# First attention: both value products of a pair of units issued in the odd step

## The chip, the cores and the metric

The kernel runs on one core of one Trainium2 chip. The metric is the device time of one execution in microseconds (us), the median of several runs. One execution is recorded by the profiler; its span runs from its first to its last instruction. TensorE is PE in the profile (PEld is its loading of weights), VectorE DVE, ScalarE ACT, GpSimd POOL and SyncE SP.

## The reference, cut to what matters

Two layers over x of shape (8, 16, 16, 192). The first is window attention with 12 heads of 16 and relative positions, and an MLP; the second causal attention with 3 heads and a soft mixture of 4 experts. The change lies in the window attention:

```python
attn = jnp.einsum('bqc,bkc->bqk', q * scale, k)
attn = (attn.reshape(-1, WS, WS, WS, WS) + rel_h[:, :, :, :, None] + rel_w[:, :, :, None, :]).reshape(-1, N, N)
attn = jax.nn.softmax(attn, axis=-1)
out = jnp.einsum('bqk,bkc->bqc', attn, v)
```

Each image of 16 x 16 tokens is padded to 28 x 28 and cut in windows of 14 x 14, so one window is full of real tokens and the three others hold two border strips and padding.

## The kernel before

The first attention is `body_a`, a loop of 4 iterations over pairs of images (`PAIRS`), between 44 and 310 us of the span. An iteration computes relative position terms and v, and then goes through 18 units (`UNITS`): 12 main ones (`MAIN`), each two heads of one image's full window (scores of 112 x 784 for four parts), and 6 border ones (two heads of both images' border, 128 x 512). Two units make a pair d; there are 9.

Every engine has its own order of the steps u; the engines meet by semaphores alone. TensorE does in step u, in this order:

- the scores of unit u (`scores_full`, L1105, or `scores_border`, L1113) into banks 0 and 1 or 2 and 3, once the exponentials of unit u-2 are done (a_p);
- the transposes of the exponentials of unit u-2 (L1207) into banks 4 and 5, once ScalarE has copied the transposes of the unit before out of them (a_pta);
- in the first three iterations, from step 18 on, query and key products of the next iteration (L222): queries in 18, 19 and 20, keys in 20;
- value products of pair d with the transposed exponentials as moving operand (`values(d, n)`, L1125 for main units, L1128 and L1131 for border ones), accumulated into bank 6 or 7. The half n adds one unit's share for both of its heads; main and border halves have 4 and 6 matmuls in the program (8 and 12 in the trace, where a matmul of f32 shows twice). The last one counts a_o up;
- in steps 5, 9 and 13 transposes of normalized tokens for the next iteration (`front_turn_part`, L1085 and L1089); the last of them only if there is one.

ScalarE does in step u the copy of unit u-2 from banks 4 and 5 to one of four buffers `pts` (L902), and then the exponentials of unit u (L912), 4 or 2 instructions; after them, in steps 5, 9 and 13, it moves the turned tokens out (L845, L849). VectorE does in step u the maxima of unit u (L638), in even steps the reciprocal of pair (u-6)/2 (`sums`, L607), in odd ones the scaling of pair (u-7)/2 (`scaled`, L620 to L626), which sets bank 6 or 7 free (a_on), and a share of the next tokens' split. Pair d is given to VectorE by a_o, and ScalarE's copy of unit v waits for a_o of pair v/2 - 2, because it reuses that buffer.

Before its value products a pair waits for v (d = 0), for the copies of both of its units, for its bank (from d = 2), and for turned tokens moved out of bank 7 (d = 1, 3, and 5 where there is a next iteration). After the last step come, in the first three iterations, two more key products, and then the projection (L1256, L1257), VectorE's residual and the next iteration.

Of the kernel before, what the change touches and what calls it, by code (L numbers as in the profile page):

```python
# [37 lines left out]
OUTS = UNITS // 2  # L38
# [30 lines left out]
def build(nc, x, xe, wall0, wall1, rel, wp, w2a, w2e, bias_cols, bias_rows, b2r, c_ident, c_keys,  # L69
          c_border, c_mask, out):  # L70
    with ExitStack() as ctx:
# [3 lines left out]
        def sem(name):  # L75
            return ctx.enter_context(nc.semaphore(name))
# [29 lines left out]
        def views(spec):  # L106
# [74 lines left out]
        ln_mv, ln_rstd, ln_xn, ln_tr, ln_tr_e, ln_xt, ln_xt_e, ln_hi, ln_split = (  # L181
            sem(n) for n in ("ln_mv", "ln_rstd", "ln_xn", "ln_tr", "ln_tr_e", "ln_xt", "ln_xt_e", "ln_hi", "ln_split"))

        a_q, a_k, a_v, a_qraw, a_ka, a_kb, a_ve, a_kae, a_rel, a_qa = (
            sem(n) for n in ("a_q", "a_k", "a_v", "a_qraw", "a_ka", "a_kb", "a_ve", "a_kae", "a_rel", "a_qa"))
# [3 lines left out]
        a_s, a_nm, a_p, a_t, a_pta, a_o, a_own, a_on = (  # L189
            sem(n) for n in ("a_s", "a_nm", "a_p", "a_t", "a_pta", "a_o", "a_own", "a_on"))  # L190
# [34 lines left out]
        def xcols(a, b):  # L225
            return [xs[:, k, a:b] for k in range(3)]
# [10 lines left out]
        def unit(u):  # L237

            if u < MAIN:
                return QR, 2, 2 * QT, u // HP, u % HP  # L240
            return P, 1, EKEYS, None, u - MAIN
# [20 lines left out]
        def gated(eng, n):  # L262

            eng.sem_inc(gate[n], 1)
# [799 lines left out]
        def _(pe):  # L1064
# [52 lines left out]
            def values(d, n):  # L1117

                rows, parts, keys, i, h = unit(2 * d)
                at, vc = n * parts * rows, slice(n * 3 * HD, n * 3 * HD + 4 * HD)  # L1120
                for k in range(2) if parts == 2 else ((2, 0, 1), (0, 1, 2))[n]:
                    for p in range(2):
                        o, turned = ps[64 * p:64 * p + 64, 6 + d % 2, :], pts[(2 * d + p) % 4]
                        if parts == 2:
                            last = mm(o[:, 0:2 * QR], ve[0:QT, 2 * i + k, h + p, vc], turned[0:QT, k, at:at + 2 * QR],  # L1125
                                      start=n + k == 0, stop=n + k == 2)
                        elif k == 2:
                            last = mm(o[:, 0:P], vee[:, 2, h + p, vc], turned[:, 1, at:at + P], start=n == 0, stop=n == 1)  # L1128
                        else:
                            part = slice(64 * k, 64 * k + 64)  # L1130
                            last = mm(o[:, part], vee[:, k, h + p, vc], turned[:, 0, at + 64 * k:at + 64 * k + 64],  # L1131
                                      start=False, stop=False)
                return last

            def queries(g):

                product(ps[:, g, :], (CQ + g * P, CQ + g * P + P), xcols(0, N)).then_inc(a_q, 1)
# [5 lines left out]
            def body_a(it, nxt):  # L1143

                pe.wait_ge(o_res, 1 + it * 2)

                pe.wait_ge(a_qraw, it * G + 3)
                gated(pe, 0)
                q4 = qraw.rearrange("p g (i t) -> p (g i) t", i=2)
                for step in range(4):  # L1150
                    if step == 1:
                        pe.wait_ge(a_ka, it + 1)
                        pe.wait_ge(a_kb, it * 2 + 1)
                    if step == 2:
                        pe.wait_ge(a_kb, it * 2 + 2)
                    if step:
                        gated(pe, 0)
                    for k in range(4):
                        at = 4 * step + k
                        for cols in range(2):  # L1160
                            rows = q4.rearrange("p a (y x) -> p a y x", x=W)
                            to = ps[:, REL_BANKS[cols][step], 0:384]
                            to = to.rearrange("p (a y k) -> p k a y", k=4, a=2 * G)[:, k] if cols else \
                                to[:, 96 * k:96 * k + 96]
                            last = mm(to, relt[:, W * cols + at, :],  # L1165
                                      rows[:, :, :, at] if cols else rows[:, :, at, :], start=True, stop=True)
                    last.then_inc(a_rel, 1)

                pe.wait_ge(a_xw, it * 3 + 3)
                for i in range(2):  # L1170

                    pe.wait_ge(a_qw, it * 4 + 1 + 2 * i)
                    gated(pe, 0)
                    for t in range(2):
                        at = N + P + (2 * i + t) * QT
                        last = product(ps[0:QT, V_BANKS[i], t * D:t * D + D], (CV, CV + D), xcols(at, at + QT), True)
                    last.then_inc(a_v, 1)
                pe.wait_ge(a_qa, it * 4 + 3)
                gated(pe, 0)
                product(ps[:, V_BANKS[2], 0:D], (CV, CV + D), xcols(N, N + P), True).then_inc(a_v, 1)  # L1180
                base = it * UNITS
                for u in range(UNITS + 4):
                    if u < UNITS:
                        rows, parts, keys, i, h = unit(u)
                        if u == 0:

                            pe.wait_ge(a_qa, it * 4 + 4)
                            pe.wait_ge(a_qw, it * 4 + 4)
                        if u >= 2:

                            pe.wait_ge(a_p, base + u - 1)
                        if u == MAIN:

                            pe.wait_ge(a_kae, it * 2 + 2)
                            pe.wait_ge(a_qb, it * 2 + 2)
                        gated(pe, 0)
                        (scores_full(u, i, h) if u < MAIN else scores_border(u, h)).then_inc(a_s, 1)
                    if 2 <= u < UNITS + 2:
                        v = u - 2
                        rows, parts, keys, i, h = unit(v)  # L1200
                        half = keys // 2

                        pe.wait_ge(a_p, base + v + 1)
                        pe.wait_ge(a_pta, 1 + base + v)
                        for k in range(2):
                            for n in range(UH * parts):
                                last = tr(ps[0:half, 4 + k, n * rows:n * rows + rows],  # L1207
                                          pp[0:rows, v % 3, n, k * half:k * half + half], ident[0:rows, 0:rows])
                        last.then_inc(a_t, 1)
                    if nxt and UNITS <= u < UNITS + G:  # L1210

                        if u == UNITS:
                            pe.wait_ge(ln_split, it + 2)
                        queries(u - UNITS)
                    if nxt and u == UNITS + 2:

                        pe.wait_ge(a_p, base + UNITS)
                        keys_of(0)
                    if u >= 4:
                        d, n = (u - 4) // 2, (u - 4) % 2  # L1220
                        if n == 0:
                            if d == 0:

                                pe.wait_ge(a_ve, it * 6 + 6)

                            pe.wait_ge(a_pta, 1 + base + 2 * d + 2)
                            if d >= 2:
                                pe.wait_ge(a_on, it * OUTS + d)

                            if d in (1, 3):  # L1230
                                pe.wait_ge(ln_xt, 2 * it + 3 + d // 2)
                            if nxt and d == 5:
                                pe.wait_ge(ln_xt_e, it + 2)
                            gated(pe, 0)
                        last = values(d, n)
                        if n:
                            last.then_inc(a_o, 1)
                    if u in ((5, 9, 13) if nxt else (5, 9)):

                        if u > 5:  # L1240
                            pe.wait_ge(a_on, 1 + it * OUTS + u // 2 - 2)
                        front_turn_part(it + 1, u // 4 - 1, (ln_xt_e, it + 1))

                if nxt:

                    pe.wait_ge(a_pta, 1 + base + UNITS)
                    for g in (1, 2):
                        keys_of(g)
                pe.wait_ge(a_on, 1 + it * OUTS + OUTS)
                project(0, (6, 7))  # L1250
# [154 lines left out]
            for w in range(CUNITS):  # L1405
                it, u = divmod(w, CU)
# [262 lines left out]
```

## Time and profile before

| | |
|---|---|
| median of 3 runs | 916.26 us (914.36 to 916.26) |
| the profiled execution | 910.88 us |
| its span | 909.0 us, mean granted clock of TensorE 0.992 |
| TensorE busy | 836.4 us, 92% of the span |
| VectorE, ScalarE, GpSimd busy | 459.0, 461.3 and 180.4 us |
| TensorE in the chain that ended last | 75% |

Busy shares are those of the whole span; the first attention takes less than a third of it. In timelines a line is a run of like instructions, with its start, its length (the end of a group of matmuls is modelled and lies some hundredths past the start of the next group), and in square brackets the idle time of the engine before it and what ended that.

### The profile page before, as it was taken

How to read it: one execution, taken by the hardware profiler on the slowest of the kernel's cores; microseconds unless marked ns; L12 is line 12 of the kernel's file. 1: busy time of each engine (PE TensorE's matmuls, PEld its weight loads, DVE VectorE, ACT ScalarE, POOL GpSimd, SP SyncE). 2: the span in 40 equal slices, each digit the busy share in tenths (PEclk: the TensorE clock that was granted, in tenths of full speed). 3: DMA queues.
4: the chain of work that ended last, by engine and by line, in shares of the span. 5: the costliest groups of instructions: out<-in, count | busy, mean ns of one | idle time of the engine just before them, and what ended most of it. 6: DMA issues, size and time to landing. Idle time of an engine off the chain costs nothing.

```text
span 909.0 us, 14872 instructions
## 1 busy us (share of the span) xinstructions
PE 836.4 (92%) x5384; PEld 675.3 (74%) x5384; DVE 459.0 (50%) x1025; ACT 461.3 (51%) x945; POOL 180.4 (20%) x257
## 2 busy tenths in 40 slices
PE   1989989989989899989988999989999899989998
PEld 1866866766776687878877599966998589975988
DVE  4878688688687643366655410264004530163001
ACT  5887677678578443246645333354343342453232
POOL 3050040031010022236302500034001420034000
PEclk9999999999999999999998999999999999999999
DMA  7010000000000000001003000000000000000000
GB/s 203 1 40 2 1 27 12 0 12 23 0 1 1 27 12 23 12 24 45 16 1 121 1 1 0 5 14 0 0 0 17 0 0 0 0 18 1 1 1 17
DMA packets 12710, 15.48 MB, mean 17 GB/s; under 512 B 5312, under 2 KB 10560, under 8 KB 12544
## 3 DMA queue, kind: packets, MB, share of 16 engines
q1 hardware_dynamic: 10656, 9.46, 3.4%
q0 software_dynamic: 2016, 5.51, 2.2%
q8 instruction: 24, 0.39, 0.2%
q14 instruction: 14, 0.11, 0.0%
HBM read 13.39 MB, written 1.57 MB: 16 GB/s over the span
## 4 chain that ended last, share of the span: by engine, by line
PE 75%; DVE 12%; ACT 5%; issue 5%; DMA 1%; SPq 0%; POOL 0%; DVEq 0%; ACTq 0%; POOLq 0%
PE ps L222 20%; PE ps L1554 14%; PE ps L1481 6%; PE ps L1207 5%; PE ps L1569 5%; PE ps L1125 4%; PE ps L1299 4%; PE ps L1105 3%; DVE area L276 2%; ACT area L912 2%; PE ps L1113 2%; PE ps L1085 1%; DVE dstat L772 1%; PE ps L1165 1%; PE ps L1511 1%
## 5 line engine op out<-in xcount | busy, mean ns | idle before, releaser
L222 PE MATMUL ps<-xs,ws 128*128 128x512 f32 x460 | 124.9, 416 | 5.7 <-DVE xs L503 3.7
L1554 PE MATMUL ps<-area 128*128 128x192 f32 x768 | 127.4, 326 | 0.0
L1554 PEld LDWEIGHTS ps<-area 128*128 128x128 f32 x768 | 124.8, 190 | 2.1 <-issue 0.5
L222 PE MATMUL ps<-ws,wx 128*128 128x512 f32 x480 | 116.1, 397 | 1.2 <-DVE ws L793 1.2
L1053 ACT ACTIVATE area<-ps,bcol 128x512 f32<-128x512 f32 x96 | 65.7, 688 | 86.6 <-PE ps L222 86.6
L804 DVE TENSOR_TENSOR area<-ps,area 128x384 f32<-128x384 f32 x32 | 17.9, 558 | 177.8 <-PE ps L1554 177.7
L222 PEld LDWEIGHTS ps<-ws,wx 128*128 128x128 f32 x480 | 89.3, 188 | 22.6 <-DVE ws L793 3.0
L222 PEld LDWEIGHTS ps<-xs,ws 128*128 128x128 f32 x460 | 86.0, 196 | 24.1 <-issue 6.4
L912 ACT ACTIVATE area<-ps,nm 112x196 f32<-112x196 f32 (+1 forms) x240 | 85.6, 440 | 19.5 <-DVE nm L638 19.5
L415 POOL TENSOR_TENSOR area<-area,dstat 128x512 f32<-128x512 f32 x32 | 32.9, 1040 | 271.4 <-DVE dstat L769 271.4
L638 DVE TENSOR_REDUCE nm<-ps 112x4 f32<-112x784 f32 (+1 forms) x72 | 62.7, 874 | 26.8 <-PE ps L1105 21.7
L1207 PE MATMUL ps<-ident,area 112*98 112x112 f32 (+1 forms) x480 | 63.0, 271 | 1.0 <-ACT room L902 0.7
L1207 PEld LDWEIGHTS ps<-ident,area 112*98 112x98 f32 (+1 forms) x480 | 46.6, 131 | 21.4 <-issue 15.0
L1481 PE MATMUL ps<-area,xn 128*128 128x512 f32 x128 | 57.5, 597 | 5.1 <-DVE area L785 4.1
L1105 PE MATMUL ps<-area 64*112 64x196 f32 x384 | 44.0, 350 | 15.5 <-ACT area L912 13.6
L607 DVE RECIPROCAL room<-ps 128x224 f32<-128x224 f32 (+1 forms) x36 | 48.6, 1351 | 12.8 <-PE ps L1128 12.6
L1105 PEld LDWEIGHTS ps<-area 64*112 64x112 f32 x384 | 30.3, 175 | 26.9 <-issue 26.9
L1481 PEld LDWEIGHTS ps<-area,xn 128*128 128x128 f32 x128 | 23.4, 190 | 31.6 <-issue 31.6
L421 POOL TENSOR_TENSOR area<-area 128x512 f32<-128x512 f32 x32 | 39.6, 1280 | 34.8 <-DVE area L785 34.8
L1569 PE MATMUL ps<-area 128*128 128x193 f32 x256 | 42.7, 326 | 0.0
L1569 PEld LDWEIGHTS ps<-area 128*128 128x128 f32 x256 | 42.1, 190 | 0.0
L902 ACT ACTIVATE area<-ps 98x896 f32<-98x896 f32 (+1 forms) x40 | 31.6, 791 | 18.8 <-PE ps L1207 18.7
(177 smaller groups left out, 1373.7 us busy)
## 6 DMA issues: line engine op xcount, KB each, us to landing
stage<-in_wall POOLq DMA_DIRECT2D x42, 128.0 KB, 2.4
area<-in_w2e SPq DMA_DIRECT2D x1, 2304.0 KB, 8.3
out<-xres SPq DMA_DIRECT2D x4, 384.0 KB, 2.6
xres<-in_x SPq DMA_DIRECT2D x1, 1152.0 KB, 7.8
area<-in_wall SPq DMA_DIRECT2D x2, 512.0 KB, 5.7
area<-in_w2a SPq DMA_DIRECT2D x1, 576.0 KB, 3.7
room<-in_rel SPq DMA_DIRECT2D x4, 128.0 KB, 5.7
xres<-in_x SPq DMA_DIRECT2D x1, 384.0 KB, 3.2
```

The costliest lines, as they stand in the source:

```text
L222: last = mm(out_, l, r, start=n == 0, stop=n == len(pairs) - 1)
L421: nc.gpsimd.tensor_tensor(ct[:, s, :], ct[:, s, :], bc, ALU.add).then_inc(d_cs, 1)
L607: V.reciprocal(den[:, d % 2, 0:n], ps[:, 6 + d % 2, 0:n]).then_inc(a_own, 1)
L638: V.tensor_reduce(nm[0:rows, u % 2, 0:UH * parts], ps[0:rows, b0:b0 + UH, 0:parts * keys].rearrange("p h (t k) -> p h t k", k=keys), AX.X, ...
L912: last = A.activation(pp[0:rows, u % 3, k, 0:keys], ps[0:rows, UH * (u % 2) + k // parts, c0:c0 + keys], ACT.Exp, bias=nm[0:rows, u % 2, k ...
L1053: A.activation(hTd[:, m, :], ps[:, (e * MC + m) % 4, :], ACT.Gelu_apprx_tanh, bias=bcol[:, E1B + e * MC + m:E1B + e * MC + m + 1]).then_in ...
L1105: last = mm(ps[0:QR, UH * (u % 2) + k, 2 * QT * t:2 * QT * t + 2 * QT], qs[q, 2 * operands(h) + i, QR * t:QR * t + QR], keys, start=True, ...
L1125: last = mm(o[:, 0:2 * QR], ve[0:QT, 2 * i + k, h + p, vc], turned[0:QT, k, at:at + 2 * QR], start=n + k == 0, stop=n + k == 2)
L1207: last = tr(ps[0:half, 4 + k, n * rows:n * rows + rows], pp[0:rows, v % 3, n, k * half:k * half + half], ident[0:rows, 0:rows])
L1481: last = mm(ps[:, 4 * h + 2 * b + part, :], xn[:, 2 * b + j, part * P:part * P + P], dd[:, b, j, 512 * h:512 * h + 512], start=j == 0, sto ...
L1554: last = mm(ps[:, 4 + b, s * D:s * D + D], hTd[:, m, b * T + s * P:b * T + s * P + P], w2x[:, e * MC + m, :], start=m == 0, stop=m == MC - 1)
L1569: last = mm(ps[:, 6 + n // 2, (n % 2) * (D + 1):(n % 2 + 1) * (D + 1)], ct[:, s, n * P:n * P + P], yy[:, n // 2, s, :], start=s == 0, stop ...
```

## The change

TensorE's value products of a pair stood in two steps: the first half in step 2d + 4, the second in step 2d + 5. Now both stand in step 2d + 5, behind that step's transposes, with the waits that stood before the first half. The even steps from 4 to 20 hold no value products. Other engines' programs are not touched.

```diff
--- before.py
+++ after.py
@@ -1216,25 +1216,23 @@
 
                         pe.wait_ge(a_p, base + UNITS)
                         keys_of(0)
-                    if u >= 4:
-                        d, n = (u - 4) // 2, (u - 4) % 2
-                        if n == 0:
-                            if d == 0:
-
-                                pe.wait_ge(a_ve, it * 6 + 6)
-
-                            pe.wait_ge(a_pta, 1 + base + 2 * d + 2)
-                            if d >= 2:
-                                pe.wait_ge(a_on, it * OUTS + d)
-
-                            if d in (1, 3):
-                                pe.wait_ge(ln_xt, 2 * it + 3 + d // 2)
-                            if nxt and d == 5:
-                                pe.wait_ge(ln_xt_e, it + 2)
-                            gated(pe, 0)
-                        last = values(d, n)
-                        if n:
-                            last.then_inc(a_o, 1)
+                    if u >= 5 and u % 2:
+                        d = (u - 5) // 2
+                        if d == 0:
+
+                            pe.wait_ge(a_ve, it * 6 + 6)
+
+                        pe.wait_ge(a_pta, 1 + base + 2 * d + 2)
+                        if d >= 2:
+                            pe.wait_ge(a_on, it * OUTS + d)
+
+                        if d in (1, 3):
+                            pe.wait_ge(ln_xt, 2 * it + 3 + d // 2)
+                        if nxt and d == 5:
+                            pe.wait_ge(ln_xt_e, it + 2)
+                        gated(pe, 0)
+                        values(d, 0)
+                        values(d, 1).then_inc(a_o, 1)
                     if u in ((5, 9, 13) if nxt else (5, 9)):
 
                         if u > 5:
```

## Rows read from the trace of the kernel before

**Rows 1.** Windows, second iteration: stretch, us, busy PE, PEld, DVE, ACT, POOL, clock, DMA.

```profile
116.00:126.00 10.00, 6.12 (x60) 4.71 (x57) 9.63 (x26) 5.80 (x15) 5.15 (x10) 1.00 0.00 0
126.00:161.00 35.00, 34.49 (x330) 22.34 (x329) 28.88 (x42) 28.48 (x64) 8.22 (x16) 1.00 0.09 25
```

**Rows 2.** Timeline, TensorE, second iteration, steps 10 and 11: start us, us, engine, line.

```profile
141.60 0.65 PE L1085 MATMUL ps<-ident,xn 128*128 128x128 f32 x4 [0.16 <-DVE area L620]
142.18 0.92 PE L1105 MATMUL ps<-area 64*112 64x196 f32 x8
143.03 0.97 PE L1207 MATMUL ps<-ident,area 112*98 112x112 f32 x8
143.93 0.98 PE L1125 MATMUL ps<-room 98*64 98x224 f32 x8
144.84 0.92 PE L1105 MATMUL ps<-area 64*112 64x196 f32 x8
145.69 0.97 PE L1207 MATMUL ps<-ident,area 112*98 112x112 f32 x8
```

**Rows 3.** Timeline, ScalarE, second iteration, the copies of steps 10 and 11.

```profile
144.12 0.92 ACT L902 ACTIVATE area<-ps 98x896 f32<-98x896 f32 x1 [0.71 <-PE ps L1207]
...
146.70 0.92 ACT L902 ACTIVATE area<-ps 98x896 f32<-98x896 f32 x1 [0.41 <-PE ps L1207]
```

**Rows 4.** Timeline, VectorE, second iteration, step 10.

```profile
143.15 0.97 DVE L638 TENSOR_REDUCE nm<-ps 112x4 f32<-112x784 f32 x1 [0.96 <-PE ps L1105]
144.04 1.55 DVE L607 RECIPROCAL room<-ps 128x224 f32<-128x224 f32 x1
```

**Rows 5.** Timeline, TensorE, second iteration, step 4.

```profile
124.81 0.92 PE L1105 MATMUL ps<-area 64*112 64x196 f32 x8 [0.24 <-ACT area L912]
...
126.57 0.98 PE L1125 MATMUL ps<-area,room 98*64 98x224 f32 x8
```

**Rows 6.** Timeline, ScalarE, second iteration, exponentials of steps 2 and 3.

```profile
123.27 1.39 ACT L912 ACTIVATE area<-ps,nm 112x196 f32<-112x196 f32 x4
...
125.85 1.37 ACT L912 ACTIVATE area<-ps,nm 112x196 f32<-112x196 f32 x4 [0.33 <-DVE nm L638]
```

**Rows 7.** Timelines, first and last iteration: values of step 4, exponentials of step 3.

```profile
54.70 0.98 PE L1125 MATMUL ps<-area,room 98*64 98x224 f32 x8
...
53.53 1.37 ACT L912 ACTIVATE area<-ps,nm 112x196 f32<-112x196 f32 x4
...
269.86 0.98 PE L1125 MATMUL ps<-area,room 98*64 98x224 f32 x8
...
268.71 1.36 ACT L912 ACTIVATE area<-ps,nm 112x196 f32<-112x196 f32 x4
```

**Rows 8.** Timeline, TensorE, second iteration, steps 14, 17 and 18.

```profile
152.68 0.66 PE L1113 MATMUL ps<-area 64*64 64x256 f32 x8
153.27 0.66 PE L1207 MATMUL ps<-ident,area 128*128 128x128 f32 x4
154.11 0.98 PE L1125 MATMUL ps<-room 98*64 98x224 f32 x8 [0.18 <-issue]
...
159.48 0.66 PE L1207 MATMUL ps<-ident,area 128*128 128x128 f32 x4
...
160.91 0.30 PE L1207 MATMUL ps<-ident,area 128*128 128x128 f32 x1 [0.17 <-ACT room L902]
```

**Rows 9.** Timeline, ScalarE, second iteration, copies of steps 14 and 17.

```profile
154.05 0.60 ACT L902 ACTIVATE area<-ps 128x512 f32<-128x512 f32 x1 [0.19 <-PE ps L1207]
...
160.17 0.60 ACT L902 ACTIVATE room<-ps 128x512 f32<-128x512 f32 x1 [0.30 <-PE ps L1207]
```

**Rows 10.** Timelines, last iteration: TensorE's step 19, VectorE's reciprocal of pair 7.

```profile
304.92 0.63 PE L1207 MATMUL ps<-ident,area 128*128 128x128 f32 x4 [0.18 <-ACT area L902]
...
306.20 0.96 DVE L607 RECIPROCAL room<-ps 128x128 f32<-128x128 f32 x1 [0.53 <-PE ps L1128]
```

**Rows 11.** Timeline, TensorE, first iteration, scores of step 2.

```profile
47.34 1.59 PE L1105 MATMUL ps<-area 64*112 64x196 f32 x8 [2.00 <-ACT area L912]
```

## The prediction

> **What bounds the kernel now.** I read the windows first. Inside the step loop of the first attention (126 to 161 us, second iteration) TensorE is busy 34.49 of 35 us at granted clock 1.00, VectorE 28.88 and ScalarE 28.48; in the ten microseconds ahead of it, where the loop fills, TensorE has 6.12 of 10 [rows 1]. So from step 4 on this stage goes at TensorE's pace, and anything that stops TensorE there is added to the time.
>
> The timeline of TensorE comes next. It shows what a step is made of: in steps 10 and 11 of the second iteration scores take 0.85 us (142.18 to 143.03), the transposes 0.90, half a pair of value products 0.91, then the next scores at once [rows 2]. Two steps are 2 x 2.66 = 5.32 us without idle time. The reader is to look at what fills the distance between one group of transposes and the next: values 0.91 and scores 0.85. All transposes write banks 4 and 5, and the transposes of unit v wait (a_pta) until ScalarE has copied unit v-1 out of these banks. The ScalarE timeline says when that is: the copy starts 1.09 us after the transposes start (143.03 to 144.12) or 1.01 (145.69 to 146.70), and lasts 0.92 [rows 2, 3]. What a copy costs up to the next transposes shows where TensorE already waits for one: copy at 160.17, 0.60 long, transposes at 160.91, so 0.14 us from its end [rows 8, 9].
>
> **The change.** Arithmetic, data and buffers stay. The same 8 + 8 value matmuls of each of the 9 pairs are issued together in the odd step; no transfer moves, and the queues of SP and POOL are not touched. Signals a_o come at the same place of the order. Per pair one half moves from between the even step's transposes and the odd step's scores to behind the odd step's transposes. The even step becomes 0.85 + 0.90 = 1.75 us, the odd one 0.85 + 0.90 + 1.82 = 3.57. No new wait is written, but an old one starts to bind.
>
> *Transposes of steps 7, 9, 11.* From the start of the even step's transposes, TensorE reaches the odd ones after 0.90 + 0.85 = 1.75 us. The copy allows them after 1.01 to 1.09, plus 0.92, plus 0.14 = 2.07 to 2.15. Wait 0.32 to 0.40, I take the middle, 0.36: these are two kinds of copy that alternate, and which falls in the even step I leave open. 3 per iteration, 4 iterations: 12 x 0.36 = 4.32 (3.84 to 4.80). Behind the waiting transposes stand both halves of the values, the token transposes and the next scores. VectorE waits for those scores: it starts its maximum 0.97 us after they start (142.18 to 143.15), and then has a reciprocal of 1.55 [rows 2, 4]. ScalarE waits for the transposes. Neither becomes the limit: both had about 6 of 35 us free and the stage gets longer.
>
> *Step 13.* The scores of the border units (step 12 on) take 0.59 (152.68 to 153.27) [rows 8], but the transposes of step 12 are still of the long kind with the long copy: 0.90 + 0.59 = 1.49 against 2.07 to 2.15. Wait 0.58 to 0.66, 4 times: 2.48 (2.32 to 2.64).
>
> *Steps 15 and 17.* Transposes 0.59, scores 0.59: 1.18. The border copy starts 0.78 (153.27 to 154.05) or 0.69 (159.48 to 160.17) after its transposes and lasts 0.60: 0.78 or 0.69 + 0.60 + 0.14 = 1.52 or 1.43 [rows 8, 9]. Wait 0.25 to 0.34, 8 times, taken 0.295: 2.36 (2.00 to 2.72). In step 19 of the first three iterations a query product lies between, and nothing waits.
>
> *Step 5.* Here ScalarE still sets the pace. Its exponentials are followed by the scores that need their bank: started 123.27, 1.39 long, scores at 124.81, so duration + 0.15 [rows 5, 6]. The scores of step 5 need the exponentials that start at 125.85 and last 1.37: they may start at 127.37. Now the first value half runs from 126.57 and fills this time; without it TensorE stands from 126.57: 0.80 us. In the third iteration all is the same to 0.01 us. In the first, 53.53 + 1.37 + 0.15 = 55.05 against 54.70: 0.35; in the last, 268.71 + 1.36 + 0.15 = 270.22 against 269.86: 0.36 [rows 7]. Sum 0.35 + 2 x 0.80 + 0.36 = 2.31.
>
> *End of the last iteration.* No queries follow there. The transposes of step 19 wait for a copy as now (0.18 idle before 304.92), and the half of pair 7 that now runs ahead of them in this gap comes after them: its reciprocal at 306.20 is on the chain that ends the stage, so it is later by the length of that half. A half of this kind runs in step 17 from 159.48 + 0.59 = 160.07 to 160.91 less the wait of 0.17: 0.67 [rows 8, 10].
>
> *What falls away.* Three waits of today. Step 9's token transposes wait 0.16 for VectorE (before 141.60) [rows 2]; in the new step they come a copy wait later, x4 = 0.64. Values in step 14 wait 0.18 for transposed tokens (before 154.11), in the first three iterations; the half is now in step 15: 0.54. Transposes of step 18 wait 0.17 for a copy (before 160.91); the whole pair now stands ahead of them, x4 = 0.68 [rows 8]. Together 1.86.
>
> *Joining the halves.* The trace has no two halves back to back. TensorE shows no idle time at the seams (143.03, 143.93, 144.84 follow on) [rows 2], so I take 0. Bounds: a gain of one wait like the 0.17 at each of 36 pairs, 6.1 us, and a loss of 0.04, the spread of the stall above, 1.4 us.
>
> **Sum.** 2.31 + 4.32 + 2.48 + 2.36 + 0.67 - 1.86 = 10.28 us; with the ends of the waits 9.3 to 11.3. After the loop the same instructions follow, and the phases between the iterations (projection, residual, relative terms) are chained to TensorE's last products, so the delay passes through whole. The profiled execution took 910.88 us (span 909.0): it would be 921.2. The runs shown have a median of 916.26, 5.4 us above it, and the change is added to that: **926.5 us, +1.1%**.
>
> **The clock, and a rule against it.** The new waits are many and short. In the fill phase TensorE idled nearly 4 of 10 us and kept clock 1.00 [rows 1]; in the first iteration, though, a group of scores took 1.59 us where later ones take 0.92 [rows 2, 11], which I read as the lower of the clock's two levels (1.2 and 2.4 GHz). The Trainium skill (TensorE: Matmul & The Clock Gate, A second HAM failure mode: psum-queue depth-cycling) says that TensorE idling briefly but often between groups while it cycles through PSUM banks can make the clock swing between its levels; the next rival is what it would do here. By its rule 932 us, by the rows 926.5. The loop of before already has such short waits, at clock 1.00.
>
> **Rivals.** *The clock falls.* If in each of the four iterations one group of scores and one of transposes run at the low level, at 1.59 - 0.92 = 0.67 us more each: 8 x 0.67 = 5.4, so 10.3 + 5.4 = 15.7: 932. Against it: the rows at clock 1.00 with more idle time than the change adds.
>
> *The joined halves run tighter.* At the bound above: 10.3 - 6.1 = +4.2, 920.5. For it: weights of the second half could be loaded under the first. Against it: no idle time at today's seams.
>
> *The copy hides anyway (the other side).* If the copy could follow the early transposes, because the order on ScalarE is what holds it until 1.01 to 1.09 us and the shorter even step brings its predecessor forward, the 24 copy waits would vanish: 2.31 + 0.67 - 1.86 = +1.1, 917.4, which is no measurable change. A measurement tells about 0.2% (1.8 us) from no change; this rival decides from the point where the 24 waits cost less than 0.7 us together, 0.03 each. Against it: the copy reads all eight transposes, and starts 0.1 to 0.2 us behind the last of them today. With the seam gain as well it would be faster, some 911.
>
> **Chances.** The forecast 0.73, own range 923.5 to 929.5 (its bounds, and some 2 us for the scatter of the runs, 914.36 to 916.26). Clock 0.09, tighter halves 0.08, hidden copy 0.10, of which 0.04 with the seam gain. Range 920.5 to 931.5: it leaves out the hidden copy, and about half of the clock's cases. Slower by over 0.2%: 0.90; within 0.2%: 0.06; faster: 0.04.
>
> **What would show it.** In the changed timeline: transposes in steps 7, 9, 11, 13, 15, 17 with idle time before them put down to ScalarE's copy (0.3 to 0.4, 0.6, 0.3 us); no such gap in even steps; scores of step 5 preceded by 0.8 us in the second and third iterations and 0.35 in the others; the gaps at step 9's token transposes and steps 14 and 18 gone; iteration length up by about 2.6 us; everything after the first attention of the same length. Wrong would be: copies starting well under 1 us after the transposes, value groups under 1.82 us for a pair, granted clock under 1.00 between steps 5 and 18, or VectorE named as what ends TensorE's waits.

## The result, and the profile after

The changed kernel takes 919.26 us (median of 20 runs, 914.64 to 923.55) against 916.02 us (20 runs, 910.48 to 919.88) on the same chips: ratio 1.0035, 95% interval 1.002 to 1.005. That is slower by 1.8 to 4.6 us, at the median 3.2, and not by 10.3. The direction was right; the size was three times too large, and the measured time lies below both ranges of the prediction.

The page of the changed kernel: span, busy time, and the granted clock in 40 slices.

```profile
span 917.7 us, 14872 instructions
...
PE 836.6 (91%) x5384; PEld 680.1 (74%) x5384; DVE 455.5 (50%) x1025; ACT 461.5 (50%) x945; POOL 180.4 (20%) x257
...
PEclk9999999999989889999998999999999999999999
```

Its span is 8.7 us longer than before's, more than the medians differ. The windows say why this one execution exaggerates (columns as in [rows 1]). Three stretches ran at a lower clock: the fill of the second iteration, the fill of the last one, and the end of the first attention with the products behind it. The third iteration's steps ran at 1.00.

```profile
116.00:126.00 10.00, 6.95 (x50) 5.39 (x52) 9.66 (x27) 5.13 (x14) 4.79 (x9) 0.83 0.00 0
201.00:236.00 35.00, 32.87 (x323) 22.25 (x323) 26.64 (x39) 27.18 (x61) 7.94 (x15) 1.00 0.06 17
266.00:276.00 10.00, 9.18 (x56) 6.92 (x56) 6.26 (x17) 6.81 (x17) 1.23 (x2) 0.66 0.00 0
312.00:331.00 19.00, 15.35 (x88) 12.97 (x85) 8.95 (x28) 4.91 (x7) 4.67 (x8) 0.73 0.16 46
```

The first costs little: the second iteration takes 73.07 us (116.31 to 189.38), the third 72.90. The two others cost some 2.3 us each. From its first scores to the projection the last iteration takes 53.85 us (262.28 to 316.13) against 50.35 before (259.32 to 309.67), of which 1.25 is the change (worked out further down). From the projection to the second large group of products behind it (L222) there are 26.45 us (316.13 to 342.58) against 24.04 (309.67 to 333.71). From there to the end the two executions differ by 0.2 us.

So the reading below uses the third iteration, steps 5 to 9, 12 and 13, and 14 and 15. TensorE's timeline of the changed kernel, which answers to [rows 2, 5, 8]:

```profile
201.04 0.92 PE L1105 MATMUL ps<-area 64*112 64x196 f32 x8 [0.73 <-ACT area L912]
201.89 0.97 PE L1207 MATMUL ps<-ident,area 112*98 112x112 f32 x8
202.79 1.73 PE L1125 MATMUL ps<-area,room 98*64 98x224 f32 x16
204.46 0.66 PE L1085 MATMUL ps<-ident,xn 128*128 128x128 f32 x4
205.04 0.92 PE L1105 MATMUL ps<-area 64*112 64x196 f32 x8
205.90 0.97 PE L1207 MATMUL ps<-ident,area 112*98 112x112 f32 x8
206.80 0.92 PE L1105 MATMUL ps<-area 64*112 64x196 f32 x8
208.05 0.94 PE L1207 MATMUL ps<-ident,area 112*98 112x112 f32 x8 [0.33 <-ACT area L902]
208.92 1.73 PE L1125 MATMUL ps<-room 98*64 98x224 f32 x16
210.59 0.92 PE L1105 MATMUL ps<-area 64*112 64x196 f32 x8
...
222.85 0.97 PE L1207 MATMUL ps<-ident,area 112*98 112x112 f32 x8
...
225.00 0.95 PE L1207 MATMUL ps<-ident,area 112*98 112x112 f32 x8 [0.58 <-ACT room L902]
...
228.50 0.66 PE L1207 MATMUL ps<-ident,area 128*128 128x128 f32 x4
...
230.02 0.63 PE L1207 MATMUL ps<-ident,area 128*128 128x128 f32 x4 [0.26 <-ACT area L902]
```

The reader sees all the waits that were forecast. Before the scores of step 5 (201.04) 0.73 us, before the transposes of step 7 (208.05) 0.33, of step 13 (225.00) 0.58, of step 15 (230.02) 0.26. From start to start the transposes lie 2.15 us apart (205.90 to 208.05) and 1.52 (228.50 to 230.02), both the figures of the prediction. The bracket is smaller than the loss by 0.07, because the modelled end of the group before counts as busy: 0.33 is a loss of 0.40.

What was not forecast stands between them: the joined pair takes 1.67 us (202.79 to 204.46, 208.92 to 210.59), where two halves took 2 x 0.91 = 1.82 [rows 2]. ScalarE answers to [rows 3]; its copy starts 1.09 us after the transposes at 205.90, as before:

```profile
206.99 0.92 ACT L902 ACTIVATE area<-ps 98x896 f32<-98x896 f32 x1 [1.06 <-PE ps L1207]
207.80 1.36 ACT L912 ACTIVATE area<-ps,nm 112x196 f32<-112x196 f32 x4
```

How long an iteration is shows from the first scores of one to the first of the next. Before and after, TensorE, third to fourth iteration:

```profile
187.53 1.58 PE L1105 MATMUL ps<-area 64*112 64x196 f32 x16 [0.34 <-issue]
...
259.32 1.58 PE L1105 MATMUL ps<-area 64*112 64x196 f32 x16 [0.34 <-issue]
```

```profile
189.38 1.58 PE L1105 MATMUL ps<-area 64*112 64x196 f32 x16 [0.35 <-issue]
...
262.28 1.58 PE L1105 MATMUL ps<-area 64*112 64x196 f32 x16 [0.35 <-issue]
```

71.79 us became 72.90: 1.11 more, and not the "about 2.6" of the prediction.

### The profile page after: what moved, and what is told of

The parts are those of the page before. It is cut to its first block, busy times and chain, and to the rows that moved or that the text cites. A ratio compares the mean times of both kernels' runs of the same rounds, so it can differ in the third digit from the quotient of the medians.

```text
span 917.7 us, 14872 instructions
## 1 busy us (share of the span) xinstructions
PE 836.6 (91%) x5384; PEld 680.1 (74%) x5384; DVE 455.5 (50%) x1025; ACT 461.5 (50%) x945; POOL 180.4 (20%) x257
## 4 chain that ended last, share of the span: by engine, by line
PE 74%; DVE 12%; ACT 6%; issue 5%; DMA 1%; SPq 0%; DVEq 0%; POOL 0%; ACTq 0%; POOLq 0%
PE ps L222 20%; PE ps L1552 14%; PE ps L1479 6%; PE ps L1207 6%; PE ps L1567 5%; PE ps L1125 4%; PE ps L1297 4%; DVE area L276 2%; PE ps L1105 2%; PE ps L1085 1%; DVE dstat L772 1%; ACT room L902 1%; ACT area L902 1%; PE ps L1165 1%; PE ps L1509 1%
## 5 line engine op out<-in xcount | busy, mean ns | idle before, releaser
L222 PE MATMUL ps<-xs,ws 128*128 128x512 f32 x460 | 125.8, 418 | 5.7 <-DVE xs L503 3.7
L222 PE MATMUL ps<-ws,wx 128*128 128x512 f32 x480 | 116.1, 398 | 1.2 <-DVE ws L793 1.2
L222 PEld LDWEIGHTS ps<-ws,wx 128*128 128x128 f32 x480 | 89.2, 188 | 22.7 <-DVE ws L793 3.0
L222 PEld LDWEIGHTS ps<-xs,ws 128*128 128x128 f32 x460 | 86.6, 197 | 24.5 <-issue 6.6
L1165 PE MATMUL ps<-area,room 128*128 128x96 f32 x256 | 36.4, 306 | 5.3 <-DVE xres L512 2.8
```

The lines of the kernel that those rows point to most:

```text
L222: last = mm(out_, l, r, start=n == 0, stop=n == len(pairs) - 1)
L1165: last = mm(to, relt[:, W * cols + at, :], rows[:, :, :, at] if cols else rows[:, :, at, :], start=True, stop=True)
```

## Experiments

In this section an iteration's length is again from the scores of unit 0 to those of the next iteration. Iterations in which groups ran at the lower clock (scores of 1.1 to 1.65 us in place of 0.92) are passed over where there is a like one to read. Experiments 1 to 4 ran on one chip and 5 to 8 on another, each set with its own runs of the kernel before beside it; the ratio and its interval are those on record and not the quotient of the two medians shown.

**1. Is the 0.15 us queue work at the seam?**

```diff
                         gated(pe, 0)
                         values(d, 0)
+                        gated(pe, 0)
                         values(d, 1).then_inc(a_o, 1)
```

> The changed kernel with one more semaphore increment of TensorE's queue (the gate that stands ahead of the first half) between the two halves. Theory A, the 0.15 us that a joined pair saves is the array's own start and drain of a group of another tile shape (the weights of a new group load only with its first matmul): the increment changes nothing, a main pair's values stay at 1.66 to 1.67 us from the first matmul to what follows, and the third iteration stays at 72.9 us. Theory B, the saving is queue work that the seam no longer carries: the pair is back at about 1.8 us and the iteration near 74.2 us.

Measured: third iteration 190.95 to 263.85, 72.90 us, the same to the hundredth. A semaphore instruction between the halves costs nothing. One run, 917.85 us. Theory B falls.

**2. Halves apart, but with cover between the transposes.**

```diff
-    scores(u); transposes(u - 2); values(d, 0); values(d, 1)   # odd step
+    scores(u); values(d, 0); transposes(u - 2); values(d, 1)
```

(The lines stand for the blocks of `body_a`; the waits of the pair move with its first half.)

> The changed kernel with the odd step's order scores, first half, transposes, second half: nothing in the even step, but 1.76 us of cover between any two groups of transposes again, and the halves apart. Theory A (copy waits 2.1 us per iteration, joining gains 0.15 per pair, waits before the scores of step 5 of 0.7): no waits for a copy before odd transposes, halves of 0.91, third iteration at 71.8 - 0.5 + 0.8 = 72.1 us, the whole within 1.0 to 1.003 of before. Theory C, the gain of the changed kernel comes from something else than the seam: the iteration is shorter than before's 71.8 by the amount of the gain, some 1.2 us.

Measured: 914.62 us (10 runs) against 913.96, ratio 1.0024 (1.0004 to 1.0044); third iteration 187.73 to 259.88, 72.15 us (72.1 expected): longer than before's 71.79, so the gain does not come from something else than the joining (theory C falls). TensorE's timeline, steps 6 and 7 of it (transposes are on L1223 here):

```profile
204.39 0.97 PE L1223 MATMUL ps<-ident,area 112*98 112x112 f32 x8
205.30 0.92 PE L1105 MATMUL ps<-area 64*112 64x196 f32 x8
206.15 0.98 PE L1125 MATMUL ps<-room 98*64 98x224 f32 x8
207.06 0.97 PE L1223 MATMUL ps<-ident,area 112*98 112x112 f32 x8
207.96 0.98 PE L1125 MATMUL ps<-room 98*64 98x224 f32 x8
```

No wait before 207.06, and each half takes 0.91 again. So the copy wait goes with the distance between two groups of transposes, and the saving goes with the joining.

**3. Take away the copy wait alone.**

```diff
-                        A.activation(pts[v % 4][0:half, :, 0:wide], ps[0:half, 4:6, 0:wide], ACT.Copy)\
-                            .then_inc(a_pta, 1)
+                        A.activation(pts[v % 4][0:half, 0, 0:wide], ps[0:half, 4, 0:wide], ACT.Copy).then_inc(a_ph, 1)
+                        act.wait_ge(a_t, base + v + 1)
+                        A.activation(pts[v % 4][0:half, 1, 0:wide], ps[0:half, 5, 0:wide], ACT.Copy).then_inc(a_pta, 1)
```

Transposes into bank 4 count a_th up, which the first copy waits for, and wait for a_ph; those into bank 5 go by a_t and a_pta.

> The changed kernel with ScalarE's copy cut in two, bank 4 and bank 5, each with its own signal both ways, so that transposes into bank 4 wait only for the first copy. ScalarE has one more instruction per unit (some 0.15 us more). Theory A: the waits before the transposes of steps 7 to 17 vanish, 2.1 us per iteration, third iteration at 70.8 us, whole time 8 us less than the changed kernel, 0.994 of before. Rival: ScalarE, at 28.5 of 35 us before, becomes the limit and the waits turn up before the scores instead; then the iteration stays over 72 us.

Measured: 908.85 us (10 runs) against 913.96, ratio 0.9953 (0.9933 to 0.9972). The first iteration went from 72.30 us (44.01 to 116.31) to 70.16 (44.35 to 114.51), 2.14 less. The waits before its odd transposes had cost 2.54 from start to start (brackets 2.09). Of these, 0.18 comes back because the six groups of transposes behind them take 0.90 us again and not 0.87, and 0.22 in steps 18 and 19, where transposes and queries take 2.23 us (87.91 to 90.14) after 2.01 (89.92 to 91.93 in the changed kernel). The third iteration had groups at the low clock, so the 70.8 expected of it can't be read. TensorE's steps 8 and 9, the copies between, and the window of the step loop:

```profile
65.36 0.97 PE L1210 MATMUL ps<-ident,area 112*98 112x112 f32 x8
66.26 0.92 PE L1106 MATMUL ps<-area 64*112 64x196 f32 x8
67.11 0.97 PE L1210 MATMUL ps<-ident,area 112*98 112x112 f32 x8
68.02 1.74 PE L1126 MATMUL ps<-area,room 98*64 98x224 f32 x16
```

```profile
66.06 0.54 ACT L902 ACTIVATE room<-ps 98x448 f32<-98x448 f32 x1 [0.80 <-PE ps L1210]
66.50 0.54 ACT L904 ACTIVATE room<-ps 98x448 f32<-98x448 f32 x1
```

```profile
56.00:88.00 32.00, 32.00 (x319) 21.68 (x316) 25.43 (x37) 26.99 (x73) 8.11 (x15) 1.00 0.07 21
```

TensorE has no idle time in 32 us. The two copies lie 0.44 us apart, and the first ends at 66.60, before TensorE comes back to bank 4 at 67.11. The edit does two things: the copy starts after half of the transposes (0.70 us behind their start, 65.36 to 66.06, and not 1.09), and it gives the banks back one by one. By the prediction's sum the earlier start alone would allow the transposes of steps 7, 9 and 11 after 0.70 + 0.92 + 0.14 = 1.76 us (an estimate), where TensorE needs 1.75, but not those of step 13 (1.49); no run separates the two. ScalarE, busy 26.99 of 32, is not the limit: the rival falls.

**4. First pair apart.**

```diff
+                    if u == 4:
+                        ...
+                        values(0, 0)
+                    if u == 5:
+                        values(0, 1).then_inc(a_o, 1)
-                    if u >= 5 and u % 2:
+                    if u >= 7 and u % 2:
```

> The changed kernel with the first pair's halves where they were, in steps 4 and 5; all other pairs joined. Theory A: the wait of 0.73 us before the scores of step 5 is gone and one seam of 0.15 is back: third iteration 72.9 - 0.6 = 72.3 us, whole time 2.3 us under the changed kernel, 1.001 of before. Rival: the wait only moves, because the exponentials of the fill phase set the pace whatever fills the gap: the iteration stays at 72.9.

Measured: 915.26 us (10 runs) against 913.96, ratio 1.0022 (0.9999 to 1.0045). Second iteration 115.98 to 188.28, 72.30 us, as expected, and no wait before the scores of step 5. The gap was idle time that the first half used to fill. The whole time alone would not tell this from no effect; the iteration does.

**5. A seam elsewhere.**

```diff
                         values(d, 0)
+                        if u in ((5, 9, 13) if nxt else (5, 9)):
+                            ...
+                            front_turn_part(it + 1, u // 4 - 1, (ln_xt_e, it + 1))
                         values(d, 1).then_inc(a_o, 1)
```

> The changed kernel with the token transposes of steps 5, 9 and 13 between the two halves of the pair and not behind them. The same work and waits, but one more change of tile shape in three steps of an iteration. Theory A (a seam costs 0.15 us wherever tiles of another shape follow): the third iteration, scores of unit 0 to scores of unit 0, goes from 72.90 to 72.90 + 3 x 0.15 = 73.35 us. Rival (the 0.15 is special to value halves with scores or transposes between): it stays at 72.9.

Measured: the third iteration had a group at the low clock. The first: 44.34 to 117.49, 73.15 us, against 72.30. Of the 0.85, 0.40 is something I had not expected: in step 9 the token transposes, now earlier, wait 0.33 for VectorE again, as in [rows 2]. The rest, 0.45, is three seams of 0.15. Step 5 of the third iteration shows one by itself:

```profile
205.35 0.98 PE L1125 MATMUL ps<-area,room 98*64 98x224 f32 x8
206.26 0.66 PE L1085 MATMUL ps<-ident,xn 128*128 128x128 f32 x4
206.84 0.98 PE L1125 MATMUL ps<-area,room 98*64 98x224 f32 x8
207.75 0.92 PE L1105 MATMUL ps<-area 64*112 64x196 f32 x8
```

0.91 + 0.58 + 0.91 = 2.40 us, where pair and token transposes in a row took 1.67 + 0.58 = 2.25 (202.79 to 205.04 above). One run, 920.23 us.

**6. Is the copy in two a gain by itself?** The edit of experiment 3 on the kernel before.

> The kernel before with ScalarE's copy cut in two, the halves of each pair apart as they were. Theory A (the cut helps only because the joined halves bared the copy): only the 0.17 us before the transposes of step 18 can go, third iteration 71.6 to 71.8 us, whole 0.998 to 1.001 of before. Rival (the cut is a gain by itself, worth the 0.5% that it showed with the joined halves): 0.995.

Measured: 911.91 us (10 runs) against 914.21, ratio 0.9991 (0.9959 to 1.0023); third iteration 187.41 to 259.04, 71.63 us, though two groups of scores in it took 1.16 and 1.49. No measurable gain, as the theory has it: the copy was hidden by the half that the change moved away.

**7. Everything together.** Experiments 3 and 4, and pair 7 apart in the last iteration:

```diff
+                    if not nxt and u == UNITS:
+                        pe.wait_ge(a_pta, 1 + base + 16)
+                        pe.wait_ge(a_on, it * OUTS + 7)
+                        gated(pe, 0)
+                        values(7, 0)
+                    if not nxt and u == UNITS + 1:
+                        values(7, 1).then_inc(a_o, 1)
```

> Joined halves and copy in two, with the first pair apart in every iteration (steps 4 and 5) and pair 7 apart in the last one (steps 18 and 19). Theory A: from the 0.9953 of the joined kernel with the copy in two, 0.55 us less in three iterations, 0.1 in the last and 0.5 to 0.6 at its end, together 2.3 us: 0.993 of before, third iteration 70.2 us without a clock dip. Rival (ScalarE and VectorE are the limit by now, the gaps only move): 0.995.

Measured: 908.48 us (7 runs) against 914.21, ratio 0.9926 (0.9899 to 0.9954), faster than both kernels. Second iteration 114.24 to 184.47, 70.23 us. Its interval overlaps that of experiment 3, so how much the two pairs apart add is shown by iterations only.

**8. The pair ahead of the odd transposes.**

```diff
-    scores(u); transposes(u - 2); values(d, 0); values(d, 1)   # odd step
+    scores(u); values(d, 0); values(d, 1); transposes(u - 2)
```

> The changed kernel with the joined pair ahead of the odd step's transposes. Now 2.5 us lie between even and odd transposes, and only the next scores between odd and even ones. Theory A (the wait follows from the distance of two groups of transposes, whichever step they stand in): no waits before odd transposes; waits for the copy before the transposes of step 8 (0.33 to 0.40), step 12 (0.58 to 0.66), step 16 (0.26) and step 18 (about 0.8, no scores there); none in 6 and 10, where token transposes of 0.59 lie between. Third iteration 72.5 to 73.1 us. Rival (the wait belongs to the odd units' buffers): waits stay in odd steps.

Measured: 926.19 us (one run); the third iteration had groups at the low clock (75.50 us), the second two groups of scores of 1.08 and 1.52 us, and 74.28: some 1 us over what I expected. There is no wait before odd transposes, and the copy waits before steps 8, 12, 16 and 18 are where they were forecast; one that was not forecast stands before step 14 (a bracket of 0.29 before 84.17). And there is a wait that I had missed, before the scores of odd steps. TensorE's steps 8 and 9 of the first iteration (transposes are on L1224), and ScalarE's beside them:

```profile
65.71 0.92 PE L1105 MATMUL ps<-area 64*112 64x196 f32 x8
66.88 0.94 PE L1224 MATMUL ps<-ident,area 112*98 112x112 f32 x8 [0.25 <-ACT area L902]
68.14 0.92 PE L1105 MATMUL ps<-area 64*112 64x196 f32 x8 [0.32 <-ACT area L912]
```

```profile
65.81 0.92 ACT L902 ACTIVATE area<-ps 98x896 f32<-98x896 f32 x1 [0.93 <-PE ps L1224]
66.63 1.36 ACT L912 ACTIVATE area<-ps,nm 112x196 f32<-112x196 f32 x4
```

The odd transposes now come 1.67 us later, so their copy on ScalarE (65.81) does too, and behind it in ScalarE's order the exponentials (66.63) that free the bank for the scores of step 9: 66.63 + 1.36 + 0.15 = 68.14. A late copy costs twice where something waits behind it.

## Why the prediction was wrong

The step that failed is "Joining the halves": "TensorE shows no idle time at the seams (143.03, 143.93, 144.84 follow on) [rows 2], so I take 0". The seams cost 0.15 us for each pair of main units (1.82 to 1.67), and 0.14 for a border pair (2 x 0.60 to 1.06, 234.90 to 235.96). The change joins 8 pairs of an iteration, 6 of them main, and not 9: 24 x 0.15 + 8 x 0.14 = 4.7 us, most of the 6.1 that the prediction gave as a bound for 36 pairs.

Its first sentence, that "the trace has no two halves back to back", is wrong too. In steps 20 and 21 nothing stands between the halves of pair 8, so the kernel before has a joined pair in every iteration. Here are the first half of pair 6 (step 16), and pair 8 with what follows, second iteration of the kernel before:

```profile
158.28 0.44 PE L1128 MATMUL ps<-area,room 128*64 128x128 f32 x4
...
158.88 0.66 PE L1113 MATMUL ps<-area 64*64 64x256 f32 x8
...
168.11 0.44 PE L1128 MATMUL ps<-area,room 128*64 128x128 f32 x4
168.38 0.64 PE L1131 MATMUL ps<-area,room 128*64 128x64 f32 x16
168.84 0.39 PE L1128 MATMUL ps<-area,room 128*64 128x128 f32 x4
169.16 2.58 PE L222 MATMUL ps<-xs,ws 128*128 128x512 f32 x10
```

A half alone takes 0.60 us (158.28 to 158.88), the pair 1.05 (168.11 to 169.16) and not 1.20. So the price of a seam could have been read before the change was made.

Groups of matmuls that follow on without a bracket can still hide a start-up, since the distance from start to start contains it. The engine that loads the weights fits this. Before (PEld, steps 10 and 11), and after (a joined pair, step 7 of the second iteration):

```profile
143.03 0.75 PEld L1207 LDWEIGHTS ps<-ident,area 112*98 112x98 f32 x8 [0.24 <-ACT area L912]
143.93 0.58 PEld L1125 LDWEIGHTS ps<-room 98*64 98x64 f32 x8 [0.15 <-issue]
144.84 0.60 PEld L1105 LDWEIGHTS ps<-area 64*112 64x112 f32 x8 [0.33 <-issue]
```

```profile
135.98 1.33 PEld L1125 LDWEIGHTS ps<-room 98*64 98x64 f32 x16 [0.15 <-issue]
137.64 0.61 PEld L1105 LDWEIGHTS ps<-area 64*112 64x112 f32 x8 [0.33 <-issue]
```

Each group, of 8 or of 16 matmuls, has its loading idle for 0.15 to 0.33 us ahead of it, and its first weights load when its first matmul starts (the same start in both timelines, to 0.01 us here); later ones load under the matmuls. 16 matmuls have that once. Experiment 1 shows that it isn't the queue's work, experiment 5 that token transposes between the halves cost the same. What in the array makes it so, the change of the tile's shape or something that goes with it, is argued and not shown: no run changed the group without changing the shape.

The other steps:

- *Copy waits in steps 7 to 17*: right in mechanism, place and size. In the first three iterations they came out at the upper bound (0.40, 0.66, 0.34), in the last at the lower (brackets of 0.25, 0.51 and 0.18 to 0.19): together 3 x 2.54 + 2.1 = 9.7 us, forecast 9.16. Experiments 2, 3, 6 and 8 bear the mechanism out.
- *Step 5*: 0.80 (bracket 0.73) as forecast in the second and third iterations' kind. The 0.35 for the first iteration was read from an execution where scores of step 2 ran 1.59 us there [rows 11]; the first iteration of the changed kernel had no such group and waited 0.74.
- *What falls away*: all three waits went, but I took the brackets, 0.16 to 0.18. From start to start each was 0.07 more, so an iteration got back 0.73 and not 0.51.
- *End of the last iteration*: forecast 0.67 for a half whose start-to-start time is 0.60. From the transposes of step 19 to the reciprocal of pair 7 there were 1.28 us [rows 10] and are 1.73 (310.93 to 312.66 in the chain): 0.45, since the joined pair is shorter.
- *Transposes after a wait* take 0.87 us up to the values (208.05 to 208.92), not 0.90, 24 times: 0.03 each that I had not counted.
- *Steps 18 and 19*: without the halves of pair 7 between them, transposes and queries take 0.12 us less (3.35 us from 235.96 to 239.31; before, 1.72 + 1.75 from 232.74 to 234.46 and from 235.06 to 236.81), three times. I had not counted that either.

For the third iteration: 0.80 + 2.54 - 0.73 - 6 x 0.15 - 2 x 0.14 - 6 x 0.03 - 0.12 = 1.13, measured 1.11. Three times 1.11 and the last iteration make 4.6 us. The last one's 1.25 is worked out from experiment 4: its last iteration takes 51.39 us from first scores to projection (before 50.35), and the joined first pair adds 0.36 - 0.15. The 0.36 is confirmed by experiment 5, whose last iteration has a bracket of 0.29 before the scores of step 5 (276.60). The ratio says 1.8 to 4.6, so the account stands at its upper end, and 1.4 us are missing to the median. Runs at different clocks lie further apart than that: of the 20 runs of the changed kernel, the four with a mean granted clock of 0.990 took 914.6 to 915.9 us, the nine with 0.984 took 918.9 to 920.0. For the 20 runs of before the clock is not on record, so what the 1.4 us are stays open.

*The clock, and the rule.* The windows of the changed kernel show 1.00 through the stretch with the new waits (201 to 236 us), and 0.83 and 0.66 in the fill phases of the second and the last iteration. Low groups turn up in the fill phase of one iteration or another, in before's first [rows 11] and also in experiment 7, which has no copy waits; this is its scores of step 2, third iteration:

```profile
188.75 1.65 PE L1106 MATMUL ps<-area 64*112 64x196 f32 x8 [2.69 <-ACT area L913]
```

So the new waits in steps 7 to 17 don't bring the clock down where they stand, and it falls without them too. Whether the changed kernel falls to the lower level more often is not settled: the mean granted clock was 0.986 over its 20 runs, and 0.988 and 0.987 over the kernel before's 25 and 18 runs on the chips of the experiments. The rule in the Trainium skill (TensorE: Matmul & The Clock Gate, A second HAM failure mode: psum-queue depth-cycling) is not borne out here for waits of 0.26 to 0.58 us, 6 in an iteration. *Tighter halves* was the rival that came true (920.5, chance 0.08), by the sign that the prediction gave: value groups under 1.82 us for a pair. *The hidden copy* fell: the copies start as late as before.

## What to carry to other kernels

Where an engine is packed, read groups from start to start: per group there is a fixed part, here 0.15 us, that no idle time shows, and joining two groups of one kind saves it. But what stood between them was cover for somebody's copy; before moving work, work out the distance between the two instructions that share a buffer, and if the cover goes, make the hand-over finer. Here joining alone lost 0.35%, a finer copy alone changed nothing that can be measured, both together gained 0.5%, and 0.7% with the first and one late pair left apart; the intervals of the last two overlap.

## What the runs showed of the hardware

- A group of matmuls in this loop has a start-up of about 0.15 us at granted clock 1.00: 8 value matmuls 0.91 us, 16 in a row 1.67.
- A semaphore increment on TensorE's queue between two groups of one kind cost nothing (72.90 us with and without).
- A ScalarE copy of 98 x 896 from two banks takes 0.92 us, and two of 98 x 448 start 0.44 us apart: with 0.87 us to the next instruction in place of 0.81, cutting it in two costs 0.06. The first bank is free 0.54 us after the copy starts and not 0.92, and the copy can start 0.4 us earlier, once the first bank is full (0.70 us behind the start of the transposes, not 1.09).
